# The experts' weights of layer 1: from SyncE's queue to ScalarE's, at other times

## The reference

```
xn = layernorm(x)
q, k, v: low-rank projections of xn, 16 heads of 8, rotary positions on half of q and k
att = softmax(causal(q @ k.T / sqrt(8)));  attention output = (att @ v) @ Wc

logits = xn @ wg                           # 128 experts
e1, e2 = the two best experts; g1, g2 = their gates, normalised
each expert takes at most 32 tokens, in order of arrival, the first choices first
buf[e, c] = the tokens of expert e;  yb[e] = buf[e] @ we[e]      # 128 matrices of 128x128
x = x + attention output + g1 * yb[e1, c1] + g2 * yb[e2, c2]
```

## Time and profile before

| | us |
|---|---|
| runs shown, median of 3 (lowest to highest) | 2201.09 (2199.76 to 2203.64) |
| the profiled execution | 2217.88 |
| its span | 2216.1 |

### The profile page before, as it was taken

How to read it: one execution, slowest core, us unless ns; L and a number is a source line. 1 busy time by engine, 2 the same in 40 slices (tenths; PEclk the granted TensorE clock), 3 DMA queues, 4 the chain that set the end, 5 groups by cost and what they waited for, 6 DMA issues and landing times. The chain is left out here.

```text
span 2216.1 us, 40363 instructions
## 1 busy us (share of the span) xinstructions
PE 1973.5 (89%) x13618; PEld 1134.9 (51%) x13618; DVE 1736.0 (78%) x2778; ACT 1343.3 (61%) x2423; POOL 1293.1 (58%) x975
## 2 busy tenths in 40 slices
PE   5799999999999999999999999948999999988886
PEld 3455555555555555555555555534555555544442
DVE  5699988998898898898888988838877677764445
ACT  3577677776776776776777777513555555534443
POOL 2486876876777867767777768643332222215540
PEclk7899999999999999999999999958999999988887
DMA  8541532523515515415335235052322222233437
GB/s 203 140 103 43 138 89 63 134 68 89 133 41 117 125 30 136 103 44 137 84 68 133 72 79 134 6 147 93 101 88 82 79 85 84 86 100 111 123 96 234
DMA packets 184476, 222.49 MB, mean 100 GB/s; under 512 B 28632, under 2 KB 122880, under 8 KB 180160
## 3 DMA queue, kind: packets, MB, share of 16 engines
q1 hardware_dynamic: 179568, 215.29, 37.8%
q0 software_dynamic: 2048, 4.18, 0.7%
q10 hardware_dynamic: 2640, 0.24, 0.1%
HBM read 165.41 MB, written 54.27 MB: 99 GB/s over the span
## 5 line engine op out<-in xcount | busy, mean ns | idle before, releaser
L732 POOL TENSOR_TENSOR dBx<-REP,BC 128x1024 f32<-128x1024 f32 x256 | 603.2, 2359 | 281.9 <-DVE dA L897 223.3
L897 DVE TENSOR_TENSOR_SCAN dA<-dA,dBx 128x512 f32<-128x512 f32 x512 | 626.2, 1223 | 108.5 <-POOL dBx L732 67.0
L404 PE MATMUL UP<-xnT,W 128*128 128x512 f32 x1024 | 518.4, 624 | 57.3 <-ACT hT L606 43.2
L413 PEld LDWEIGHTS DN<-W,hT 128*128 128x128 f32 x4096 | 469.7, 192 | 110.9 <-issue 100.6
L413 PE MATMUL DN<-W,hT 128*128 128x128 f32 x4096 | 496.4, 278 | 0.3 <-ACT GD L613 0.3
L597 ACT ACTIVATE dA<-REP,A 128x512 f32<-128x512 f32 x512 | 354.2, 695 | 89.9 <-DVE PR L906 81.7
L606 ACT ACTIVATE hT<-UP,b 128x512 f32<-128x512 f32 x512 | 355.2, 694 | 75.1 <-PE UP L404 67.9
L906 DVE TENSOR_TENSOR PR<-dA,BC 128x512 f32<-128x512 f32 x512 | 353.6, 691 | 31.5 <-DVE dA L897 18.8
L404 PEld LDWEIGHTS UP<-xnT,W 128*128 128x128 f32 x1024 | 179.3, 194 | 284.5 <-issue 146.5
L1802 DVE TENSOR_REDUCE NM<-S 128x4 f32<-128x1024 f32 (+1 forms) x192 | 234.2, 1220 | 113.0 <-PE S L1355 44.5
L1557 ACT ACTIVATE PT<-S 128x1024 f32<-128x1024 f32 x192 | 196.8, 1025 | 111.0 <-PE S L1377 52.5
(11 more groups left out here) (256 smaller groups left out, 2768.3 us busy)
## 6 DMA issues: line engine op xcount, KB each, us to landing
BC<-s_b SPq DMA_DIRECT2D x128, 256.0 KB, 6.4
REP<-s_dx SPq DMA_DIRECT2D x124, 256.0 KB, 7.5
REP<-s_delta SPq DMA_DIRECT2D x124, 256.0 KB, 8.0
s_parts<-SPL SPq DMA_DIRECT2D x32, 384.0 KB
s_dx<-tz SPq DMA_DIRECT2D x16, 512.0 KB, 3.1
s_y<-zeros SPq DMA_DIRECT2D x32, 256.0 KB, 5.2
YC<-s_y SPq DMA_DIRECT2D x16, 512.0 KB, 5.6
s_delta<-soft SPq DMA_DIRECT2D x32, 255.0 KB, 3.1
```

The lines of the kernel that those rows point to most:

```text
L404: nc.tensor.matmul(UP[k % 2][:], W1[:, e % E0, f * P:(f + 1) * P], xnT[:, q, :], start=True, stop=True).then_inc(upf.sem, 1)
L413: last = nc.tensor.matmul(DN[:, j * P:(j + 1) * P], hT[:, e % 2, f, j * P:(j + 1) * P], W2[:, e, f, :], start=(f == 0), stop=(f == FB - 1))
L732: nc.gpsimd.tensor_tensor(dBx[:, s % 2], DX[:, h, j:j + 2, :], BC[:, q // 2, q % 2, :].unsqueeze(1).to_broadcast([P, 2, T0]), ALU.mult).th ...
L897: nc.vector.tensor_tensor_scan(h, h, dBx[:, k // 2 % 2, k % 2, :], 0.0, ALU.mult, ALU.add).then_inc(scan_done.sem, 1)
```

## The change

All eight loads of `WE` are taken off SyncE and issued by ScalarE. Batches 0, 1 and 2, for which the buffers are free from the start, are issued at half-steps 12 * 8 + 7, 12 * 10 + 7 and 12 * 12 + 7, that is 103, 127 and 151, fourteen, thirteen and twelve sequences earlier in the list than before. Batch b + 3 is issued at the half-step at which ScalarE scales the products of batch b (305 + 10 b), behind the wait for these products (`applied`), which it has there anyway, and ahead of the scaled copies. The transfers themselves, their sizes, the buffers and the semaphores on which TensorE waits stay as they are.

```diff
--- before.py
+++ after.py
@@ -1179,7 +1179,7 @@
     ACT_AT = dict(xT=-20, cs=(-12, -9), v=-1, spl=(-15, -12), nm=13, exp=18, osb=(26, 32), yT=39)
     DVE_AT = dict(top=-15, mk=-13, loc=(-11, -9), oh=-8, add=-2, t1=-18, t2=-15, mx=1, nms=12, epi=(34, 35), x=42)
     POOL_AT = dict(norm=-23, keep=-13, val=-5, qk=-15, r1=-13, spl=-11)
-    SP_AT = dict(xn=-14, parts=-11, load=-6, nm=12, nm_in=15, we=-17)
+    SP_AT = dict(xn=-14, parts=-11, load=-6, nm=12, nm_in=15)
     MAPPED = HS1 * (NSEQ - 1 - AHEAD)
     GATHER = MAPPED + 8
     EVERY = 10
@@ -1243,11 +1243,6 @@
             sp.sem_inc(s.sem, LEAD * s.per)
 
         yv, ov = y_d.rearrange("(c i p) d -> p c i d", c=2, p=P), out.rearrange("(i p) d -> p i d", p=P)
-
-        def weights(b):
-            if b >= WBUF:
-                sp.wait_ge(applied, b - WBUF + 1)
-            sp.dma_start(WE[:, b % WBUF], dram["L1_ffn_we"].rearrange("e d f -> d e f")[:, 16 * b:16 * b + 16, :]).then_inc(we_loaded[b % WBUF], 16)
 
         def load(q, dst, n, m):
 
@@ -1276,9 +1271,6 @@
                 sp.wait_ge(parts_out.sem, parts_out.at(n, 16))
                 load(1, KS, n, m)
                 load(0, QS, n, m)
-            for b in range(BATCHES):
-                if now == MAPPED + SP_AT["we"] + HS1 * b:
-                    weights(b)
             for n, m in due(SP_AT["nm"]):
                 sp.wait_ge(nm_copied.sem, nm_copied.at(n, 1))
                 sp.dma_start(nm_d[m], NMT[:]).then_inc(nm_out.sem, 16)
@@ -1522,6 +1514,9 @@
         act.wait_ge(stat_step, 7)
         nc.scalar.activation(stats[:, :, 0], q1[:], ACT.Sqrt).then_inc(root_done, 1)
 
+        def weights(b):
+            nc.scalar.dma_start(WE[:, b % WBUF], dram["L1_ffn_we"].rearrange("e d f -> d e f")[:, 16 * b:16 * b + 16, :]).then_inc(we_loaded[b % WBUF], 16)
+
         def half(due, ahead, now):
             for n, m in ahead(ACT_AT["xT"]):
                 act.wait_ge(fr_x.sem, fr_x.at(n, 1))
@@ -1562,6 +1557,9 @@
                         act.wait_ge(parts_out.sem, parts_out.at(n - 1, 16))
                     nc.scalar.copy(SPL[:, k], (QK if k == 0 else R1)[:]).then_inc(part_done.sem, 1)
 
+            for b in range(WBUF):
+                if now == HS1 * (8 + 2 * b) + 7:
+                    weights(b)
             for b in batch(6, now):
                 act.wait_ge(grouped, b + 1)
                 if b:
@@ -1571,6 +1569,8 @@
                 nc.scalar.activation(wsl[:, b % 2], wsl[:, b % 2], ACT.Exp).then_inc(wexp, 1)
             for b in batch(9, now):
                 act.wait_ge(applied, b + 1)
+                if b + WBUF < BATCHES:
+                    weights(b + WBUF)
                 act.wait_ge(weighed, 3 * b + 3)
                 if b >= YBUF:
                     act.wait_ge(scattered[b % YBUF], 64 * (b // YBUF))
```

## The result

| | before | after |
|---|---|---|
| median of 7 runs each, us | 2202.97 (2199.76 to 2206.58) | 2220.62 (2214.12 to 2225.42) |
| ratio after / before | | 1.0078 [1.0059, 1.0098] |
| profiled execution, us (its span) | 2217.88 (2216.1) | 2223.28 (2221.5) |

The change makes the kernel 17.2 us slower by the ratio; forecast were 15.4 us (2216 for the changed kernel). So the comparison is made stage by stage, and the steady steps carry the most weight: from the first pass of sequence 8 to that of 20, three executions without weights there take 237.5, 237.9 and 238.1 us.

A forecast was written before the change was run, and what follows sets the result against it. Two DMA engines carrying the lopsided K/Q blocks were taken to bound each load; 18.6 steady + 3.0 late - 6.2 gained = +15.4 us on a median of 2201.09 gave 2216, range 2196 to 2225.

The forecast's parts named there:

- What bounds the kernel: Layer 1 K/Q block loads: two of sixteen DMA engines limit the whole load, 13.69 us of a 19.7 us step.
- A steady step with weights: Loads of sequences 9, 11, 13: 4.2 us longer load plus 2.0 of slow TensorE clock, 6.2 each, +18.6 in all.
- 2.7 for service and 1.5 for crowding: Steady load: 2.7 us moving weights on the two engines, 1.5 from block packets slowed while all engines move.
- The reason given for it: Steady loads: on ScalarE's queue weights no longer wait behind SyncE's blocks; the two queues take turns on each engine.
- B: Rival: one order for both queues, or blocks first; a steady weight load costs 3.2 us; +4.0, 2205 us; chance 0.20.
- C: Rival: steady weights use idle engines and packet gaps without making blocks late; -5.7, 2195 us; chance 0.18.
- A: The forecast itself: queues take turns, steady weights delay the blocks; +15.4 us, 2216, own range 2209 to 2225; chance 0.60.
- D: Rival: ScalarE's issue waits for SyncE's descriptors, delaying the exponential; at most 0.7 x 3; no separate chance given.
- The late gains: Weights leaving SyncE's late queue: steps 23, 24 and 30 gain 3.2, 2.0 and 1.0 us, 6.2 in all.
- The late costs: Five late ScalarE issues: +0.5 at load 26, +2.0 for weights 7, +0.5 for ScalarE's delay; +3.0 together.
- the +0.5: Load 26 with weights 3: 4.2 us longer, less some 2 of VectorE cover and the old weights' 1.5; bounds 0 to 1.5.
- the sign that the forecast named: Sequence 29: load start to first pass up by some 1.5 us or more.

The follow-up runs named there:

- e6: Kernel before with the 16-row block of each K/Q half cut into two of 8 rows; ratio 0.9867, -29.5 us.
- e10: Kernel before with weights 0 to 2 as six 0.5 MB halves from ScalarE at slot 7, in six loads; 3 to 7 unmoved; 1.0075, +16.5 us.
- e3: Kernel before with weights 0 to 2 issued from SyncE behind the blocks of sequences 9, 11, 13; 3 to 7 unmoved; ratio 1.0012.
- e9: Kernel before with weights 0 to 2 issued from ScalarE at slot 10, behind the blocks of 9, 11, 13; 3 to 7 unmoved; ratio 1.0025.
- e4: Kernel before with weights 0 to 2 issued from ScalarE at slot 2, ahead of the loads of 9, 11, 13; 3 to 7 unmoved; ratio 0.9999.
- e1: Kernel before with only the steady part of the change: weights 0 to 2 from ScalarE at slot 7, 3 to 7 unmoved; 1.0070, +15.5 us.
- e5: Kernel before with all eight weight loads issued from ScalarE at slot 2, ahead of a load; ratio 0.9998.
- e2: Kernel before with only the late part of the change: weights 3 to 7 from ScalarE, 0 to 2 unmoved; 1.0021, +4.7 us.
- e7: Changed kernel with the 16-row block cut into two of 8 rows; against the kernel before 0.9909, -20.2 us.
- e8: Kernel before with the 16-row block cut in two and all eight weight loads from ScalarE at slot 2; 0.9812, 2162.61 us, -41 us.
- e11: As e4, but weights 3 to 7 never loaded, their products using those of 0 to 2; against the kernel before 0.9953, -10.4 us.

## Why the prediction was right

**What bounds the kernel.** Right, as far as the traces and e6 can show it: the fullest engines set the length of a load. Cutting one block has the last of it there 2.5 us earlier, takes the wait away and 29.5 us off the kernel (e6), with the bytes unchanged.

**A steady step with weights.** Forecast 4.2 of load and 2.0 of clock, 6.2 in all; measured 4.5 (18.2 - 13.7) and 2.2 (8.2 - 6.0), 6.7 in all, three times, 20. The stage from 8 to 20 as a whole is 18.8 longer, 18.6 were forecast. That the two sums agree so well is in part luck: the forecast took 5.98 for every step, but the kernel before has a slow stretch of its own behind sequence 11 (7.39), so that the clock costs 5.3 us more than before and not 6.7; against that the load of 12 is 0.7 longer. One input was off: the weights were issued at +2.7 and not at +3.9, since here the issue on ScalarE began 0.06 us after the activation ahead of it. What +3.9 would have cost, no run shows. And I had made the delay of two parts, 2.7 for service and 1.5 for crowding. e10 shows a delay that goes with the bytes (2.0 for half), which fits if both do; no run separates them.

**The reason given for it.** Half right. The forecast says that the weights stop waiting *because* they change queues. Then weights from ScalarE's queue should cost more than weights from SyncE's at whatever time they are issued. What the runs show: in e3 the weights are behind the blocks in one queue, in e9 they are in another and overlap the last blocks, and the loads are equal (15.1 and 15.0). What sets the cost is when the weights are issued, here 2.7 us into a load that has 11 more us to go. The queue was only the means by which they could be issued there: in SyncE's program the twelve blocks are ahead.

**Rivals.** B (+4.0) and C (-5.7) are both out by the ratio and by each of the three loads. C is not absurd, though: its condition, a load with weights that isn't late, is what e4 has, five slots (6 us) earlier. For A over B the forecast had little to go by: the packets of q10 in the earlier trace rows come to 0.00 MB, so they are tiny ones, and say little about 1 MB beside large blocks. D: nothing; ScalarE's next instruction isn't late.

**The late gains, 6.2.** The loads of sequences 23 and 24 are back at 13.74 and 13.42, as forecast, and the stage from 22 to 26 is 90.8 us, where it was 96.8. e1 and e3, with the same three loads gone from there, have 91.0 and 91.6. In the medians the gain is less sure: e1 is 15.5 slower with a steady part of +18.3, which leaves 2.8; e3 is at +2.7 with +9.0, which leaves 6.3; e4 is at -0.2 with -1.3, which leaves nothing. So it lies between 0 and 6. The profiled executions of e4 and e5 are 7.6 and 6.7 us below the medians of their own runs, so their traces flatter them; what the median has that the traces haven't is open.

**The late costs, 3.0.** By the traces too small, by the medians not shown to be. e2 alone, against its own runs of before, costs 4.7 [1.3, 8.0], an interval with the 3.0 in it, and the change costs 17.2 where e1, its steady part alone, costs 15.5. In the traces load 26 got 17.60 us: the 2 us of cover by VectorE, on which the +0.5 rested, belonged to the profiled execution of before; in the changed kernel's the first pass waits for the DMA, 4.22 us. Load 29 takes 16.82, where before had 15.92; 1.5 or more was the sign that the forecast named. From 22 to the end it is 269.9 us, against 263.2 in e9, which has the same batches on SyncE. Some of that is behind the last sequence: from the first pass of 31 to the end 63.6 us, 61.0 in e9, 59.9 in e10; e2, with the same late issues, has 58.1. What makes the end longer isn't settled.

**The account.** 18.8 from the steady part, so -1.6 for all the rest makes the measured 17.2; the forecast had 18.6 and -3.2. The sum is right to 2 us. The time itself, 2216 against a median of 2220.62, is 4 us low, of which 2 are the median of before, 2202.97 of seven runs where three had 2201.09.

## What to carry to other kernels

Before a transfer is moved "beside" a load, ask which DMA engines limit that load, not how busy the sixteen are on average: the share was 0.13 to 0.24, and 1 MB still made the load 4.5 us longer. Here the same transfer was free 3 us ahead of the load, made it 1.3 us longer when issued behind its blocks, and 4.5 us longer in its midst; try the place before the queue. When a wait has the share of one or two engines, look first at spreading the load's own blocks (29.5 us here for one line, where no place for the weights gave more than noise by itself). In the steady part each stall of 3 us or more was also paid a second time in TensorE's clock.

## What the runs showed of the hardware

**The price of the clock.** In the steady part of the changed kernel and of e1, with an idle time of 5.5 us and more before the first pass, each first pass with weights began at a granted clock of 0.50, and the work up to the next load took 1.3 to 2.5 us more. After 3.2 to 3.8 us (e10) it took 1.4 to 2.6 more. At 2.6 to 3.1 us it goes both ways: e3 pays 1.4 to 2.5 us three times, e9 pays 2.6 us behind 2.64 of idle time and nothing behind 2.90, twice. After 1.3 to 2.2 us there is mostly none, but now and then a slow stretch too, with weights near (e7, +1.3 after 2.19; e9, +1.3 after 1.82) and without (before, +1.4 after 1.61).

**Issue and activation.** ScalarE's DMA issue began 0.06 us after the activation ahead of it, which took 1.02 us, had begun. On ScalarE the two instructions of an issue took 0.02 and 0.70 us, on SyncE 0.21 and 0.78.

**A late part that differs between chips.** The profiled execution of before is 17 us above the median of its other runs. Its waits from 2000 to 2160 us (engine and line, what for; us in total, times, longest) have entries whose releaser the trace can't name. They are, in the second execution of before (e0):

```profile
DVE NM L1802 <- remote: 15.5, 4, 4.4
DVE rec L1785 <- remote: 13.8, 3, 5.3
ACT OSB L1551 <- remote: 12.5, 3, 5.1
ACT PT L1557 <- remote: 8.8, 3, 4.1
```

The traces of e1 to e7 were taken beside runs of before with medians of 2217 to 2221 us; from the first pass of 26 to that of 31 they take 124 to 134 us. The traces of the changed kernel and of e8 to e11 have no such entry in that window and take 104 to 116 us there; before had medians of 2202.97 and 2202.88 beside them. The kernel before itself, unchanged, has medians of 2216.87 to 2220.87 us on the one chip and 2202.88 on the other: 14 to 18 us of its time hang on the chip or the occasion. That these lie in the late part, and are the 16.8 us by which the forecast came down from its profiled execution, is argued from the traces of other kernels; there is none of the kernel before on the faster chip. In that window the kernel gathers and scatters with indirect DMAs; whether these are the cause wasn't tested. A late part should be compared only between executions of one chip. The forecast took its cover at load 26 from such a trace, and in the changed kernel's trace it wasn't there.
